# Copies of the turned exponentials of two attentions moved from ScalarE to VectorE, with a new weave and new filler counts

## What is computed

```
x = x + tanh(g_xattn[0]) * _L0_xattn_ref(_layernorm(x), ctx, ctx, mask, w_q, w_k, w_v, w_o, b_o)
...
qh, kh, vh = 16 heads of width 8, from x (queries) and ctx (keys, values)
score = einsum('bhqd,bhkd->bhqk', qh, kh) / sqrt(8);  masked entries get -inf
out   = einsum('bhqk,bhkd->bhqd', softmax(score), vh) -> (B, S, 128) @ w_o.T + b_o
```

## Time and profile before

| | us |
|---|---|
| median of 3 runs | 2598.35 |
| lowest and highest | 2594.41, 2606.62 |
| the profiled execution, whole | 2615.43 |
| its span, first to last instruction | 2613.4 |
| PE, DVE, ACT busy in the span | 2329.8, 1580.6, 1411.8 |

### The profile page before, as it was taken

One profiled execution on the slowest core, in us unless ns is written; L12 is line 12 of the kernel. 1 busy time (PEld: TensorE's weight loads), 2 busy tenths in 40 slices (PEclk: granted clock), 3 DMA queues, 4 the chain that ended last, 5 costly groups with the idle time before them and its releaser, 6 DMA issues.

```text
span 2613.4 us, 51527 instructions
## 1 busy us (share of the span) xinstructions
PE 2329.8 (89%) x19938; PEld 1626.1 (62%) x19938; DVE 1580.6 (60%) x5307; ACT 1411.8 (54%) x3970; POOL 143.7 (5%) x180
## 2 busy tenths in 40 slices
PE   5999889998899888999899998998989989899887
PEld 2668556675566755667556775567755676565765
DVE  3754666547666376664756647556475565755656
ACT  4376264753647436475365744557345573455734
POOL 0000100001000010000100001000100001000010
PEclk9999999999999899999999999999999999999999
DMA  3024000340004300043000420005200051000510
GB/s 156 1 66 114 9 13 1 80 99 17 5 1 100 80 15 7 1 100 80 17 5 1 111 69 17 5 1 122 58 17 5 1 138 42 19 3 9 137 35 5
DMA packets 312292, 115.19 MB, mean 44 GB/s; under 512 B 268737, under 2 KB 295361, under 8 KB 311793
## 3 DMA queue, kind: packets, MB, share of 16 engines
q1 hardware_dynamic: 312048, 111.90, 17.0%
HBM read 63.64 MB, written 48.23 MB: 43 GB/s over the span
## 4 chain that ended last, share of the span: by engine, by line
PE 52%; DVE 24%; ACT 9%; DMA 7%; issue 4%; POOL 3%; SPq 1%; DVEq 0%; ACTq 0%
PE banks L462 5%; PE banks L406 5%; PE banks L343 5%; ACT PP L820 3%; PE banks L292 3%; DVE nm L1163 2%; PE banks L546 2%; POOL mv L1682 2%; PE banks L340 2%; PE banks L430 2%; PE banks L573 2%; PE banks L679 2%; DMA mix_d<-gs 2%; PE banks L354 2%; DMA o_d<-oa 2%
## 5 line engine op out<-in xcount | busy, mean ns | idle before, releaser
L820 ACT ACTIVATE PP<-banks,nm 128x128 f32<-128x128 f32 x1568 | 450.3, 397 | 171.6 <-DVE nm L1163 117.4
L1163 DVE TENSOR_REDUCE nm<-banks 128x4 f32<-128x512 f32 (+1 forms) x400 | 260.0, 675 | 309.3 <-PE banks L343 263.7
L406 PE MATMUL banks<-w_sb,PP 128*128 128x128 f32 x1536 | 248.2, 285 | 44.4 <-ACT PP L827 24.5
L827 ACT ACTIVATE PP<-banks 128x512 f32<-128x512 f32 (+1 forms) x400 | 242.2, 613 | 63.2 <-PE banks L406 48.3
L292 PE MATMUL banks<-identb 128*128 128x256 bf16 x1632 | 267.4, 288 | 7.2 <-ACT PP L978 4.5
L406 PEld LDWEIGHTS banks<-w_sb,PP 128*128 128x128 f32 x1536 | 166.4, 142 | 138.4 <-ACT PP L827 90.9
L1682 POOL TENSOR_TENSOR mv<-mv,half 128x2 f32<-128x2 f32 x160 | 115.5, 722 | 2278.9 <-DVE mv L1060 2278.9
L292 PEld LDWEIGHTS banks<-identb 128*128 128x128 bf16 x1632 | 161.0, 104 | 68.0 <-issue 26.4
L462 PE MATMUL banks<-w_sb,qk 128*128 128x128 f32 x1280 | 193.4, 287 | 1.3 <-DVE qk L1298 1.3
L462 PEld LDWEIGHTS banks<-w_sb,qk 128*128 128x128 f32 x1280 | 162.9, 191 | 30.3 <-issue 11.4
L811 ACT ACTIVATE xnT<-banks 128x256 f32<-128x256 f32 x128 | 48.8, 381 | 191.0 <-PE banks L300 191.0
(11 more groups left out here) (281 smaller groups left out, 4329.0 us busy)
## 6 DMA issues: line engine op xcount, KB each, us to landing
va<-v_d SPq DMA_DIRECT2D x32, 512.0 KB, 4.1
o_d<-oa SPq DMA_DIRECT2D x64, 256.0 KB, 3.9
va<-o_d SPq DMA_DIRECT2D x32, 512.0 KB, 4.1
pv_d<-PP SPq DMA_DIRECT2D x32, 256.0 KB, 2.1
oa<-pv_d SPq DMA_DIRECT2D x32, 256.0 KB, 3.6
v_d<-PP SPq DMA_DIRECT2D x16, 512.0 KB, 4.6
v_d<-tmp SPq DMA_DIRECT2D x16, 512.0 KB, 5.6
w_sb<-weights SPq DMA_DIRECT2D x1, 5603.0 KB, 23.1
```

What stands on the lines that cost most here:

```text
L406: e = pe.transpose(bank(k, 2)[:, cols(j)], P[k][:, 512 * (u % 2) + 128 * j:][:, 0:128], ident)
L820: e = act.activation(P[k][:, 512 * (u % 2) + 128 * j:][:, 0:128], bank_[:, cols(j)], ACT.Exp, bias=nm[k][:, m:m + 1])
L827: act.activation(PT[k][:, 512 * (u % 2):512 * (u % 2) + maps * 128], bank(k, 2)[:, 0:maps * 128], ACT.Copy).then_inc(pT_ok[k], 1)
L1163: e = dve.tensor_reduce(m, b3(scores[:, 0:maps * 128], maps), AX.X, ALU.max, negate=True)
```

## The change

In both small attentions the copies of the turned exponentials leave ACT: `act_map_turned` goes out of `act_small_attention` and a `tensor_copy` with the same waits and the same increment comes into `dve_small_attention`, two behind each second maximum. All five tables of beats, `TURN` and `SHIFT` are new, and `SPARES` holds 101 products in place of 102, at other places. Nothing else differs.

```diff
-TURN, SHIFT = 36969, 1327
+TURN, SHIFT = 38499, 1336
 BEATS_PE = (
-    -182, 118, 349, 498, 1075, 1176, 1237, 2027, 2123, 2171, 2444, 2444, 2654, 2704, 2704, 2930, 3255, 3515, 3772, 3866,
...
+    -513, -157, -55, 106, 576, 862, 952, 1423, 1468, 1468, 1468, 1468, 1864, 1994, 2115, 2338, 2601, 2917, 3031, 3145, 3498,
...
@@ act_small_attention
                 if u < 8:
                     yield
                     act_map(act, k, i, 8 * s + u, u, bank(k, u % 2), HQ)
-                if u >= 1:
-                    yield
-                    act_map_turned(act, k, i, 8 * s + u - 1, u - 1, HQ)
                 if u == 5:
                     yield
                     gather_out(0)
@@ dve_small_attention
             for u in range(8):
                 yield
                 dve_max(dve, k, i, 8 * s + u, 4 * (u % 4), bank(k, u % 2), HQ, s == 0)
+                if u % 2:
+                    for n in (u - 1, u):
+                        yield
+                        dve.wait_ge(pT_ps[k], pT_ps.n(i, 8 * s + n))
+                        if n >= 2:
+                            dve.wait_ge(o_ps[k], o_ps.n(i, 8 * s + n - 2))
+                        dve.tensor_copy(PT[k][:, cols(n % 2, 512)], bank(k, 2)).then_inc(pT_ok[k], 1)
```

More of the change, by code:

```diff
@@ L34 @@
 A0, M0, A1, SW, ML, CF, WA, M3 = range(8)
-TURN, SHIFT = 36969, 1327
+TURN, SHIFT = 38499, 1336
 BEATS_PE = (
[11 rows of a table removed]
-BEATS_ACT = (
[8 rows of a table removed]
-BEATS_DVE = (
[9 rows of a table removed]
[11 rows of a table added]
+BEATS_ACT = (
[7 rows of a table added]
+BEATS_DVE = (
[10 rows of a table added]
 BEATS_POOL = (
-    27431, 31808, 38506, 41212, 45983, 49391, 49473, 58713, 61236, 62609, 62964,)
+    37787, 46200, 48362, 51739, 54157, 59453, 60519, 66029, 68063, 74327, 74375,)
 BEATS_SP = (
-    -62751, -62751, -62537, -62209, -62209, -62209, -61544, -61544, -61231, -60422, -55101, -41685, -40827, -40465, -39341,
-    -38684, -38682, -38188, -37526, -37372, -34978, -32982,)
+    -101793, -101758, -101758, -101348, -100948, -100948, -100772, -100772, -100708, -100411, -84331, -69509, -68575,
+    -67885, -67874, -67233, -67230, -66516, -66497, -66228, -64738, -63409,)
 SPARES = (
[3 rows of a table removed]
[3 rows of a table added]
 XN_A0, XN_M0, XN_A1, XN_SW, XN_ML, XN_CF, XN_WA, XN_WA2, XN_M3 = range(9)
```

## The result

The changed kernel takes 2626.4 us (median of 7 runs, 2616.7 to 2648.3) against 2598.35: the ratio is 1.0114, with an interval of 1.0087 to 1.0141, a small loss but clear of the scatter. The forecast of 2578 us had the wrong sign, and 2626 lies above its range. The profiled execution took 2640.64 us against 2615.43.

The account below looks back on a forecast made before the run. It took PE as the bound (52% of the chain), with time returning only where PE waits or does useless work; -8 - 8 + 4 - 12.5 + 5.6 - 7 + 6 = -20 us gave a 2578 us median, range 2545 to 2622.

Parts of the forecast that it names:

- The copy's price: One 512-column copy out of a bank on DVE: 0.68 us, against 0.623 us on ACT.
- Copies on the path, -8: Small attentions: five copies on the chain a turn become three, on DVE; -1.0 us a turn, -8 us.
- ACT's queue, -8: Small attentions: exponentials no longer queue behind ACT's waiting copies; a quarter of 32 us, -8 us.
- place 3: Second attention: lane 1 turns units 0 and 1 back to back, the copy between them uncovered on PE; +6 us.
- The rest, 0: First turn, other blocks' order, SP's stores and the wider shift of PE's chunks: 0, the shift within +-8 us.
- DVE's queue, +4: Small attentions: maxima, and exponentials after them, wait behind copies on DVE; +4 us, bounds 0 and +49.
- maxima behind copies: Rival, chance 0.20: on DVE nine maxima a turn are each held for a full copy; slower, 2623 us.
- Filler, -12.5 and +5.6: 30 constant products a turn leave the two attentions, -12.5 us; 28 come in elsewhere, +5.6 us.
- Place 1, -7: PE's wait for a lane's first exponentials, now covered by nine products, not four: -7 us, bounds 0 and -9.
- The clock: Rival, chance 0.05: fewer fillers or unbridged waits lower TensorE's clock; +27 us on the forecast, 2605 us.
- signs of "wrong": Later maxima, PE waiting over 2 us a window for copies, clock under 0.97, or difference in blocks without copies, among others.
- signs of "right": ACT falls, DVE rises about 10 us a window; copies 0.65-0.70 us; attentions 2-3 us shorter a turn; exponentials' wait not longer.

Follow-up runs that it names:

- e9: Kernel before with ACT's copies of turned exponentials in the small attentions cut to 64 of 512 columns: 2593 us, ratio 0.9969.
- e8: Changed kernel with DVE's copies of turned exponentials in the small attentions cut to 64 of 512 columns: 2633 us, ratio 1.0125.
- e14: Changed kernel with each copy on DVE behind the next maximum, not in pairs, and cut to 64 of 512 columns: 2632 us.
- e15: Changed kernel's order with the copies back on ACT in pairs and cut to 64 of 512 columns: 2634 us.
- e3: Changed kernel with the table of constant products (SPARES) of the kernel before: 2663 us, ratio 1.025.
- e7: Changed kernel with each copy on DVE behind the next maximum instead of in pairs, at full length: 2699 us.
- e5: Kernel before with only the changed kernel's table of constant products (SPARES): 2637 us, ratio 1.016.
- e4: Changed kernel with SyncE's (SP's) beats of the kernel before: 2645 us, ratio 1.018.
- e11: Kernel before with 13 more constant products a turn in lane 1, filling PE's gap ahead of the convolution's turns: 2606 us, ratio 1.0014.
- e10: Changed kernel with 11 more constant products a turn, filling PE's 1.32 us gap in the last mixture's weighed sum: 2629 us, ratio 1.010.
- e13: Changed kernel with two gaps filled by constant products, in the last mixture's weighed sum and ahead of the convolution's turns: 2616 us, ratio 1.0038.

## Why the prediction was wrong, step by step

- **The copy's price** was right: 0.68 forecast, 0.689 measured. The Trainium skill's figure for VectorE out of PSUM ("VectorE: DVE Perf Modes", the TRN2 errata) gives 0.66 for 512 columns, 0.03 under the row.
- **Copies on the path, -8, and ACT's queue, -8.** This step failed. I took three copies on the path at DVE's price and ACT's 4 us of waiting as a gain, and no new wait of PE. PE's wait for the moved copies went from some 6 us to 20. e9 took 96 of the 159 us of their length off ACT, and 8 us came back, 12 at equal clock; e8 shows that their length on DVE is worth 16. That makes about +4 (16 less 12, for slightly different cuts), and it holds what place 3 costs. ACT's queue alone wasn't tested, but the trace speaks against the gain: the exponentials' idle time for maxima grew as ACT emptied (all idle time before L820: 171.6 us before, 230.7 after).
- **The rest, 0.** This failed too, and it is the larger part of the waits. The new order inside the attentions makes PE wait for exponentials right behind their scores, 1.31 us twice in the first attention of a turn. No term of the sum had such a wait. In all, PE waits 35.5 us for exponentials at L406 against 17.9, and 42.6 for layer norms against 22.4. Both stay with short copies, on DVE or ACT (e8, e14, e15), and with the old products (e3), so they come with the beats. Which of the tables does it is open.
- **DVE's queue, +4.** In the new order, short copies in pairs are no worse than behind the next maximum or on ACT (2633, 2632, 2634), so there is no sign of a larger price. But the forecast treated the copies as an edit to the old order. There the queue costs 117 us and the copies' length 130 more (83 and 52 at clock 1.000). The rival "maxima behind copies" gave the measured time within 4 us, 2623 against 2626, and that is luck: it counted nine maxima held by a whole copy each, and e7 and e8 show in the changed kernel no more than a few us of such waits. DVE's idle time ahead of maxima, my argument against, is time in which PE isn't ready for DVE; it doesn't say that DVE is free when PE is.
- **Filler, -12.5 and +5.6.** The way of pricing failed: at equal clock the new table costs 24 us in the old order (e5) and saves 16 in the new one (after against e3). Filler fills the gaps of one order; a count times a share of the chain doesn't price it.
- **Place 1, -7.** This was right. The wait of 1.06 us ahead of a turn's first turned maps is gone in every turn but the first. I had the cover too small: the nine products take 2.5 us there, not 1.3, and the ones before took 1.2, not 0.4. In the trace each product of L462 shows as two matmuls, and I took the time of one for the whole.
- **Place 3, +6.** This was right too: PE waits 0.79 us between the two units in each turn, 6.3 us in all. **SP, 0:** e4 shows its new order to be no loss.
- **The clock** (0.05). Its chance was too low: some 10 of the 26 us, where the rival had 27. I looked at the attention windows, where the clock is 1.00; the fall came in a block that the copies don't touch, with a few chunks of PE's order that I had counted at 0.

At equal clock, by estimates with a few us of scatter each, the sum reads: copies +4, new order and products +12 (e8's 2574 less e9's 2562), in place of -20; and the clock +10. The +12 is a difference of runs and not a sum of waits that were seen. Of the signs of "wrong", time did arise where no copy is: four turn ends are 4 us longer each. PE waiting for copies for over 2 us a window didn't come (1.1 and 1.4), nor a clock under 0.97. Of the signs of "right", the copies' row and DVE's rise came, but exponentials are waited for longer and the two attentions are 3.2 us longer a turn, not shorter.

## What to carry to other kernels

Before counting an operation's move to an idler engine as a gain, cut it short where it stands: what comes back (8 us here, for 60% of the length) says more than shares of the chain. Look at a wait block by block, too: a sum over the span can hold another block's waits. Operations that wait for another engine don't fit into a strict queue without a new order of everything around them, and the new order has a price of its own. In a schedule with fillers, look at the lengths of TensorE's gaps as well as at their sum; neither predicts the clock by itself.

## What the runs showed of the hardware

- The clock doesn't follow from TensorE's gaps alone. With some 6 us idle in 34, in pieces up to 0.83 us, it stayed at 2.4 GHz in all turn ends of the kernel before; with nearly the same gaps it fell for 6.8 us in three turn ends of e11. With pieces of 1.39, 1.21 and 1.32 us it fell for 10 to 14 us in four of seven and stayed in three. With the last of these filled it fell in none (e10), or for 3.4 us in four (e13).
- Shorter work need not be faster: e8 saves 16 us at equal clock and loses them to the clock, 0.972 against 0.984.
- A copy of 64 columns out of a bank takes 0.22 us on DVE (e8) and one of 512 takes 0.69; on ACT it is 0.24 (e9) and 0.62.
